# Moving the PSUM evacuation and the squares of y in a two-convolution image kernel, with one more step of lag

## The chip, the cores and the metric

The kernel runs on one core of one Trainium2 chip. The metric is the device time of one execution in microseconds (us); of several executions the median is given, and smaller is better.

## The reference

Eight images of 32 channels and 192 x 192 pixels go through two residual blocks. Each block first normalizes its input over groups of two channels (mean and variance over both planes).

```python
x = x + _L0_conv_ref(_gn(x), w_off, b_off, w_dcn, b_dcn)
x = x + _L1_conv_ref(_gn(x), w1, b1, w2, b2)
# _L0: a 3x3 conv to 2 offsets for each channel, sampling of the plane at the
#      shifted place by bilinear interpolation, then a 3x3 conv over 32 channels
# _L1: pooled = x.mean(axis=(2, 3)); hdn = relu(pooled @ w1 + b1)
#      kernels = (hdn @ w2 + b2).reshape(b, NK, 3, 3); depthwise 3x3 conv with them
```

An offset is below 1 pixel in size, so that the bilinear sample lies between a pixel and one of its direct neighbours in each direction. Which neighbour it is depends on the offset's sign: hence the predicated copies.

## The kernel before

An image is cut into 12 chunks of 16 rows (`CHUNKS = 12`, `TOTAL = 96` chunks in all); 4 rows by 32 channels lie on the 128 partitions, so that a chunk is 4 x 192 elements in each partition. Every engine has its own program, written out as a loop `for i in range(STEPS)`, and semaphores tie them together. Step i of an engine works on several chunks at different distances behind i. A step's number within its image is o = i mod 12, and i = 12 b + o.

TensorE (PE) does in step i: `offsets(i, 0)` and `offsets(i, 1)`, the two halves of the offset convolution into the PSUM tile `z`; `depthwise(i - DW_STEP, 0)`, the second block's convolution into `dw`; `deform(i - 3, 0)`, the first block's second convolution into bank 0 of `dc`; then `depthwise(.., 1)` and `deform(i - 3, 1)` into bank 1. `deform(n, q)` waits on the semaphore `y_done` until bank q has been read out for chunk n - 1. Between these stand a few small matmuls for the statistics of the images: `y_means`, `hidden`, `taps` and `y_bias` (one chain after the last chunk of an image, up to the weights `wy` of the second block), and `x_mean`, `x_var`, `x_biases` for the image to come.

ScalarE (ACT) does in step i: `x_sums` (the sums of one of eight tiles `st` of the next image, loaded by DMA), at times a read of a small result (`read`), then `offset(i, 0)` (tanh of `z` to `du`), `side(i, 0)` (its sign to the mask `mu`), `y_square(i - 4)` (the sum of squares of y over chunk i - 4, which waits for `y_done`), `size(i, 0)`, the same three for the second half (`dv`, `mv`), `finish` for bank 0 of the depthwise result (`ot<-dw`), `sides(i + 1)` (a copy of the neighbours to `nb`), `finish` for bank 1. `depthwise` has one bank `dw` for all but the last image, so each half waits for the `finish` of the half before it.

VectorE (DVE) does in step i `sample(i)` and then `evacuate(i - 3)`. `sample` begins with the large predicated copy (L703, `nb<-mu,xv`, 12 x 190 elements per partition), which needs `mu`; then come two small ones of 768 elements (L710 and L711), which need `mv`, and six tensor_tensor operations up to `sr` (L731). `evacuate(n)` adds `dc`, a bias and the residual into the ring `yr`, for each of two banks, and each time counts `y_done` up by one.

SyncE (SP) issues the DMAs in the order of its own loop: the store of the output, `s_shift`, the loads of x, `st` and the residual, and `y_shift`. GpSimd (POOL) sets borders and does the small arithmetic of the normalizations (`y_norm`, `y_weights`). With `DW_STEP = 19` the second block runs 19 steps behind the first, and `yr` is a ring of `YS = 17` chunks. Steps 0 to 18 have no depthwise work; steps 96 to 114 have no offsets or sampling.

Of the kernel before, what the change touches and what calls it, by code (L numbers as in the profile page):

```python
# [16 lines left out]
B, H, W = 8, 192, 192  # L17
# [10 lines left out]
CNT = HW // G  # L28
STILES = 8
SW = HW // G // STILES  # L30
XS, SS, YS, HS = 3, 3, 17, 4
ABOVE, MID, BELOW = 0, 1, 2
BANK = 512
Q = 2
# [9 lines left out]


DCN_STEP = 3
DW_STEP = 19
STEPS = TOTAL + DW_STEP

TAPS = Q * 2 * 2 * 2  # L50
# [16 lines left out]


def s_dmas(n):
    return 2 + (n % CHUNKS % SS == 0 and n % CHUNKS > 0)  # L70


def r_dmas(n):
# [38 lines left out]
def block_kernel(nc, x, planes, w_off, b_off, w_dcn, b_dcn, w1, b1, w2, b2, consts, xr, out):  # L112
    with ExitStack() as ctx:
# [237 lines left out]
        def _(pe):  # L351
# [112 lines left out]
            def y_means(b):  # L464
                pe.wait_ge(y_tot, b + 1)
                average("ym", b, C_YM, yn[:, 0:2])
# [31 lines left out]
            for i in range(STEPS):  # L498
                b, o = divmod(i, CHUNKS)
                c, d = i - DW_STEP, i - DCN_STEP  # L500
                if i < TOTAL:
                    offsets(i, 0)
                    offsets(i, 1)
                if 0 < b <= B and o == 7:
                    y_bias(b - 1)
                if c >= 0:
                    depthwise(c, 0)
                if 0 <= d < TOTAL:
                    deform(d, 0)
                if 0 < b <= B and o == 5:  # L510
                    taps(b - 1)
                if c >= 0:
                    depthwise(c, 1)
                if 0 <= d < TOTAL:
                    deform(d, 1)
                if 0 < b <= B and o == 3:
                    y_means(b - 1)
                if 0 < b <= B and o == 4:
                    hidden(b - 1)
                if b + 1 < B:  # L520
                    if o == 9:
                        x_mean(b + 1)
                    if o == 10:
                        x_var(b + 1)
                    if o == 11:
                        x_biases(b + 1)

        @block.scalar
        def _(act):
# [122 lines left out]
            for i in range(STEPS):  # L652
                b, o = divmod(i, CHUNKS)
                c, e = i - DW_STEP, i - DCN_STEP - 1
                if b + 1 < B and 0 < o <= STILES:
                    x_sums(b + 1, o - 1)
                    if o == STILES:
                        x_totals(b + 1)
                if 0 < b <= B and o == 4:
                    read("ym", b - 1, mvy[:], sm[:, C_YM:C_YM + 2])  # L660
                if 0 < b <= B and o == 5:
                    hidden_read(b - 1)
                if 0 < b <= B and o == 6:
                    read("tap", b - 1, tapr[:], sm[:, C_TAP:C_TAP + TAPS])
                if b + 1 < B and o == 10:
                    read("xm", b + 1, mx[(b + 1) % 2][:], sm[:, C_XM:C_XM + 1])
                if b + 1 < B and o == 11:
                    read("xv", b + 1, vx[:], sm[:, C_XV:C_XV + 1])
                if 0 < b < B and o == 0:
                    off_bias(b)  # L670
                if i < TOTAL:
                    offset(i, 0)
                    side(i, 0)
                if 0 <= e < TOTAL:
                    y_square(e)
                if 0 < b <= B and o == 3:
                    y_totals(b - 1)
                if i < TOTAL:
                    size(i, 0)
                    offset(i, 1)  # L680
                    side(i, 1)
                    size(i, 1)
                if 0 < b <= B and o == 7:
                    wait(act, o_done, Q * CHUNKS * (b - 1))
                    read("wb", b - 1, wb[:], sm[:, C_WB:C_WB + Q], bias=mvy[:, 0:1])
                    act.wait_ge(small_rd, SMALL["wb", b - 1] + 1)
                if c >= 0:
                    finish(c, 0)
                if i + 1 < TOTAL:
                    sides(i + 1)  # L690
                if c >= 0:
                    finish(c, 1)

        @block.vector
        def _(dve):
            def sample(n):
                b, j = divmod(n, CHUNKS)
                s, v, q, k = n % 2, xv[n % XS], nb[n % 2], s_at(n)
                at = n * LERPS
                dve.wait_ge(sided, n + 1)  # L700
                dve.wait_ge(prepped, 4 * n + 1)
                m3 = mu[s][:].bitcast(U16).unsqueeze(1).to_broadcast([P, 3, NB, W])
                nc.vector.copy_predicated(q[:, :, :, 1:W - 1], m3[:, :, :, 1:W - 1],  # L703
                                          v[:, :, :, 3:W + 1]).then_inc(lerp, 1)
                m1 = mv[s][:].bitcast(U16)
                dve.wait_ge(prepped, 4 * n + 3)
                if j in (0, CHUNKS - 1):
                    dve.wait_ge(mirror, 2 * b + 1 + (j > 0))
                dve.wait_ge(lerp, at + 1)
                nc.vector.copy_predicated(v[:, ABOVE, :, 1:W + 1], m1, v[:, BELOW, :, 1:W + 1]).then_inc(lerp, 1)  # L710
                nc.vector.copy_predicated(q[:, ABOVE], m1, q[:, BELOW]).then_inc(lerp, 1)  # L711


                two, own = q[:, ABOVE:MID + 1], v[:, ABOVE:MID + 1, :, 1:W + 1]
                u2 = du[s][:].unsqueeze(1).to_broadcast([P, 2, NB, W])
                dve.wait_ge(lerp, at + 3)
                nc.vector.tensor_tensor(two, two, own, ALU.subtract).then_inc(lerp, 1)  # L717
                dve.wait_ge(lerp, at + 4)
                dve.wait_ge(prepped, 4 * n + 4)
                nc.vector.tensor_tensor(two, two, u2, ALU.mult).then_inc(lerp, 1)  # L720
                dve.wait_ge(lerp, at + 5)
                nc.vector.tensor_tensor(two, two, own, ALU.add).then_inc(x_free, 1)  # L722
                dve.wait_ge(x_free, n + 1)
                nc.vector.tensor_tensor(q[:, ABOVE], q[:, ABOVE], q[:, MID], ALU.subtract).then_inc(lerp, 1)  # L724
                dve.wait_ge(lerp, at + 6)
                nc.vector.tensor_tensor(q[:, ABOVE], q[:, ABOVE], dv[s][:], ALU.mult).then_inc(lerp, 1)  # L726
                wait(dve, dcn_mm, 2 * (n - 2))
                if n >= SS:
                    dve.wait_ge(s_sh[n % SS], ring(n - SS, SS, s_dmas))
                dve.wait_ge(lerp, at + 7)  # L730
                nc.vector.tensor_tensor(sr[:, k:k + NB, 1:W + 1], q[:, ABOVE], q[:, MID], ALU.add)\  # L731
                    .then_inc(sampled, 1)

            def evacuate(n):
                b, j = divmod(n, CHUNKS)
                k = y_at(n)
                dve.wait_ge(r_in[n % YS], ring(n, YS, r_dmas))
                if j == 0:
                    dve.wait_ge(small_rd, SMALL["ob", b] + 1)
                for q in range(Q):  # L740
                    y = yr[:, k:k + NB, q, 1:PAIRS + 1]
                    dve.wait_ge(dcn_mm, Q * n + q + 1)
                    nc.vector.scalar_tensor_tensor(  # L743
                        out=y, in0=dc[:, q, 0:NB * PAIRS].rearrange("p (k w) -> p k w", w=PAIRS),
                        scalar=db[b % 2][:, q:q + 1], in1=y, op0=ALU.add, op1=ALU.add,
                        accum_out=ys1[b % 2][:, q, j:j + 1]).then_inc(y_done, 1)

            dve.wait_ge(cleared, 4)
            dve.wait_ge(piv, 1)
            for i in range(STILES):  # L750
                dve.wait_ge(first_in[i], 16)
                wait(dve, first_sum, i)
                nc.vector.scalar_tensor_tensor(
                    out=st[0][:], in0=first_tile(yr, i), scalar=npiv[:],
                    in1=zero[:, 0:1].to_broadcast([P, SW]), op0=ALU.add, op1=ALU.add,
                    accum_out=xs1[:, i:i + 1]).then_inc(first_sum, 1)

            for i in range(STEPS):
                if i < TOTAL:
                    sample(i)  # L760
                if 0 <= i - DCN_STEP < TOTAL:
                    evacuate(i - DCN_STEP)

        @block.gpsimd
        def _(pool):
# [161 lines left out]
            for i in range(STEPS):  # L927
# [10 lines left out]
                    set_s_pads(i)  # L938
                if b + 1 < B and o == 0:
                    pivot(b + 1)  # L940
                if 0 < b <= B and o == 4:
                    y_norm(b - 1)
                    set_y_pads(b - 1)
                if b >= 2 and o == 5:
                    set_y_edges(b - 2)
                if 0 < b <= B and o == 6:
                    y_weights(b - 1)
                if b < B and o == 6:
                    edge_weights(b)
# [78 lines left out]
```

## Time and profile before

| | |
|---|---|
| Median of 3 runs | 1628.83 us (1628.58 to 1629.97) |
| Profiled execution, its own time | 1630.0 us |
| Its span on the core | 1628.2 us |
| TensorE matmul busy | 1535.3 us (94%) |
| VectorE busy | 1359.2 us (83%) |
| ScalarE busy | 1053.2 us (65%) |
| GpSimd busy | 326.2 us (20%) |
| Mean busy share of the DMA engines, main queue | 63.0% |

The span runs from the first to the last recorded instruction of the core. A row of the timeline names the start, the length, the engine, the line, the tiles (written before the arrow, read behind it), and in brackets how long the engine had been idle and what released it. Only an idle engine that others wait for costs time, so the shares above don't say by themselves what bounds the kernel: the stages have to be looked at one by one.

### The profile page before, as it was taken

Reading aid. Unit: us, or ns where it says so; the run is one execution under the profiler, and the core shown is the slowest. Engines: PE = TensorE matmul, PEld = TensorE weight load, DVE = VectorE, ACT = ScalarE, POOL = GpSimd, SP = SyncE. Lnnn points to the kernel's source line nnn. Section 1 sums busy time; section 2 is a strip of 40 time slices with the busy share of each in tenths; the row PEclk is TensorE's granted clock in tenths of the full one; section 3 lists DMA queues with packets and bytes.
Section 4 is the critical chain, followed back from the end, with each engine's and each line's share of the span. In section 5 each row is a group of like instructions: output and inputs, shape, how many; then the busy total and the mean of one; then the engine's idle time right before and its main releaser. Section 6 shows DMA issues by size and latency. Waiting matters only on the chain.

```text
span 1628.2 us, 29952 instructions
## 1 busy us (share of the span) xinstructions
PE 1535.3 (94%) x12048; PEld 644.3 (40%) x12048; DVE 1359.2 (83%) x1264; ACT 1053.2 (65%) x1594; POOL 326.2 (20%) x382
## 2 busy tenths in 40 slices
PE   3788888999999999999999999999999999999888
PEld 1333334434444344433444344433444334443343
DVE  3899999988988888899988989898888989889700
ACT  4767567666686667776677666766676665655423
POOL 3000422104030230404121040312304041210010
PEclk9899999999999999999999999999999999999999
DMA  7365455576676658676676766766676765656356
GB/s 243 107 190 176 113 160 176 173 209 178 208 219 201 192 173 237 185 221 191 185 223 199 213 177 209 217 203 192 173 239 187 216 189 158 189 159 199 111 149 218
DMA packets 225274, 307.78 MB, mean 189 GB/s; under 512 B 16656, under 2 KB 167552, under 8 KB 225136
## 3 DMA queue, kind: packets, MB, share of 16 engines
q1 hardware_dynamic: 223632, 304.42, 63.0%
q8 instruction: 95, 1.56, 0.4%
q0 software_dynamic: 1504, 1.45, 0.3%
q14 instruction: 43, 0.35, 0.1%
HBM read 190.18 MB, written 38.14 MB: 140 GB/s over the span
## 4 chain that ended last, share of the span: by engine, by line
PE 65%; DVE 14%; ACT 9%; DMA 4%; issue 4%; SPq 2%; POOL 1%; DVEq 0%; ACTq 0%; POOLq 0%
PE z L357 31%; PE dc L397 16%; PE dw L427 11%; DMA st<-in_planes 3%; DVE nb L722 2%; DVE nb L720 2%; DVE nb L717 2%; ACT dv L536 2%; PE dc L427 2%; ACT mv L543 1%; DVE xv L710 1%; PE dc L401 1%; DVE nb L724 1%; DVE nb L726 1%; DVE nb L711 1%
## 5 line engine op out<-in xcount | busy, mean ns | idle before, releaser
L357 PE MATMUL z<-xv,wos 128*64 128x384 f32 x4608 | 769.2, 490 | 11.1 <-ACT du L536 10.9
L357 PEld LDWEIGHTS z<-xv,wos 128*64 128x64 f32 x4608 | 327.9, 137 | 425.7 <-issue 414.4
L397 PE MATMUL dc<-sr,wds 128*32 128x384 f32 x2304 | 448.2, 520 | 35.8 <-DVE yr L743 35.7
L397 PE MATMUL dc<-sh,wds 128*32 128x384 f32 x2112 | 406.7, 521 | 0.0
L703 DVE COPY_PREDICATED nb<-mu,xv 128x2280 f32<-128x2280 uint16 x96 | 269.6, 2808 | 59.7 <-ACT mu L543 59.1
L427 PE MATMUL dw<-yr,wy 128*64 128x388 f32 x672 | 252.4, 497 | 11.6 <-ACT ot L571 9.2
L427 PE MATMUL dw<-yh,wy 128*64 128x388 f32 x672 | 252.5, 497 | 0.0
L536 ACT ACTIVATE du<-z,ob 128x768 f32<-128x768 f32 x96 | 86.1, 897 | 240.8 <-PE z L357 218.3
L397 PEld LDWEIGHTS dc<-sr,wds 128*32 128x32 f32 x2304 | 122.9, 110 | 298.1 <-issue 297.5
L557 ACT ACTIVATE nb<-xv 128x2292 f32<-128x2292 f32 x96 | 202.6, 2110 | 0.4 <-DVE sr L731 0.3
L710 DVE COPY_PREDICATED xv<-mv,xv 128x768 f32<-128x768 uint16 x96 | 103.1, 1074 | 87.0 <-ACT mv L543 64.5
L722 DVE TENSOR_TENSOR nb<-nb,xv 128x1536 f32<-128x1536 f32 x96 | 169.6, 1766 | 3.3
L720 DVE TENSOR_TENSOR nb<-nb,du 128x1536 f32<-128x1536 f32 x96 | 169.2, 1763 | 3.3
L717 DVE TENSOR_TENSOR nb<-nb,xv 128x1536 f32<-128x1536 f32 x96 | 168.9, 1759 | 3.3
L579 ACT ACTIVATE st<-st,npiv 128x1152 f32<-128x1152 f32 x56 | 70.3, 1256 | 120.8 <-DMA st<-in_planes 98.6
L427 PEld LDWEIGHTS dw<-yr,wy 128*64 128x64 f32 x672 | 83.4, 136 | 151.1 <-issue 93.2
L590 ACT ACTIVATE junk<-yr,nmx 128x768 bf16<-128x768 f32 x96 | 89.4, 931 | 66.3 <-DVE yr L743 66.0
L743 DVE SCALAR_TENSOR_TENSOR yr<-dc,db,yr 128x384 f32<-128x384 f32 x192 | 110.5, 612 | 21.7 <-DMA yr<-in_xr 9.9
L571 ACT ACTIVATE ot<-dw,wb 128x388 f32<-128x388 f32 x168 | 96.6, 575 | 39.8 <-PE dw L427 39.4
L397 PEld LDWEIGHTS dc<-sh,wds 128*32 128x32 f32 x2112 | 113.4, 111 | 3.0 <-issue 3.0
L731 DVE TENSOR_TENSOR sr<-nb 128x768 f32<-128x768 f32 x96 | 93.0, 969 | 12.5
L711 DVE COPY_PREDICATED nb<-mv,nb 128x768 f32<-128x768 uint16 x96 | 100.4, 1046 | 0.0
(118 smaller groups left out, 1586.0 us busy)
## 6 DMA issues: line engine op xcount, KB each, us to landing
xv<-in_x SPq DMA_DIRECT2D x272, 384.0 KB, 4.7
yr<-in_xr SPq DMA_DIRECT2D x96, 392.0 KB, 7.8
out<-ot SPq DMA_DIRECT2D x96, 388.0 KB, 4.3
yh<-yr SPq DMA_DIRECT2D x179, 196.0 KB, 7.2
st<-in_planes SPq DMA_DIRECT2D x56, 576.0 KB, 7.1
sh<-sr SPq DMA_DIRECT2D x160, 194.0 KB, 2.8
sh<-sr SPq DMA_DIRECT2D x32, 145.5 KB, 2.5
yr<-in_planes SPq DMA_DIRECT2D x8, 576.0 KB, 10.3
```

What stands on the lines that cost most here:

```text
L357: last = nc.tensor.matmul(acc[m], weights[:, kx, :], view[:, :, kx:kx + W], start=kx == 0, stop=kx == 2)
L397: last = nc.tensor.matmul(dc[m, q, 0:NB * PAIRS], weights[:, kx, q], view[:, :, cols], start=first, stop=final)
L427: last = nc.tensor.matmul(acc[m], wy[b % 2][:, q, t], view[:, :, t:t + OW], start=t == 0, stop=t == 1)
L536: nc.scalar.activation(d[:].rearrange("p (h k) w -> p h (k w)", h=2), z[:, i, :, 0:HALF * W], ACT.Tanh, bias=ob[b % 2][:, i:i + 1], scale= ...
L557: nc.scalar.activation(nb[s][:, :, :, 1:W], v[:, :, :, 1:W], ACT.Copy)
L703: nc.vector.copy_predicated(q[:, :, :, 1:W - 1], m3[:, :, :, 1:W - 1], v[:, :, :, 3:W + 1]).then_inc(lerp, 1)
L710: nc.vector.copy_predicated(v[:, ABOVE, :, 1:W + 1], m1, v[:, BELOW, :, 1:W + 1]).then_inc(lerp, 1)
L711: nc.vector.copy_predicated(q[:, ABOVE], m1, q[:, BELOW]).then_inc(lerp, 1)
L717: nc.vector.tensor_tensor(two, two, own, ALU.subtract).then_inc(lerp, 1)
L720: nc.vector.tensor_tensor(two, two, u2, ALU.mult).then_inc(lerp, 1)
L722: nc.vector.tensor_tensor(two, two, own, ALU.add).then_inc(x_free, 1)
L743: nc.vector.scalar_tensor_tensor(out=y, in0=dc[:, q, 0:NB * PAIRS].rearrange("p (k w) -> p k w", w=PAIRS), scalar=db[b % 2][:, q:q + 1], i ...
```

## The change

Four things change together. (1) The evacuation that VectorE did at the end of step i - 1 is now done in step i, between the large predicated copy and the two small ones. (2) ScalarE's `y_square`, and `y_totals` with it, go from the middle of the step to its end. (3) Everything in the statistics of the next image's planes (`x_sums`, `x_totals`) and the chain from `y_means` to `y_bias` is one step later. (4) The lag of the second block goes from 19 to 20 steps, and its ring from 17 to 18 chunks. Beside these, the number of DMAs that `s_dmas` gives for the first chunk of an image is 3 in place of 2, which is what `s_shift` issues there.

```diff
-XS, SS, YS, HS = 3, 3, 17, 4
+XS, SS, YS, HS = 3, 3, 18, 4
-DW_STEP = 19
+DW_STEP = 20
 def s_dmas(n):
-    return 2 + (n % CHUNKS % SS == 0 and n % CHUNKS > 0)
+    return 2 + (n % CHUNKS % SS == 0)
...
@@ tensor
-                if 0 < b <= B and o == 7:
+                if 0 < b <= B and o == 8:
                     y_bias(b - 1)
                 if c >= 0:
                     depthwise(c, 0)
                 if 0 <= d < TOTAL:
                     deform(d, 0)
-                if 0 < b <= B and o == 5:
+                if 0 < b <= B and o == 4:
+                    y_means(b - 1)
+                if 0 < b <= B and o == 6:
                     taps(b - 1)
...
-                if 0 < b <= B and o == 3:
-                    y_means(b - 1)
-                if 0 < b <= B and o == 4:
+                if 0 < b <= B and o == 5:
                     hidden(b - 1)
...
@@ scalar
-                if b + 1 < B and 0 < o <= STILES:
-                    x_sums(b + 1, o - 1)
-                    if o == STILES:
+                if b + 1 < B and 1 < o <= STILES + 1:
+                    x_sums(b + 1, o - 2)
+                    if o == STILES + 1:
                         x_totals(b + 1)
...
                 if i < TOTAL:
                     offset(i, 0)
                     side(i, 0)
-                if 0 <= e < TOTAL:
-                    y_square(e)
-                if 0 < b <= B and o == 3:
-                    y_totals(b - 1)
...
                 if c >= 0:
                     finish(c, 1)
+                if 0 <= e < TOTAL:
+                    y_square(e)
+                if 0 < b <= B and o == 3:
+                    y_totals(b - 1)
...
@@ vector
                 nc.vector.copy_predicated(q[:, :, :, 1:W - 1], m3[:, :, :, 1:W - 1],
                                           v[:, :, :, 3:W + 1]).then_inc(lerp, 1)
+                if 0 <= n - DCN_STEP - 1:
+                    evacuate(n - DCN_STEP - 1)
                 m1 = mv[s][:].bitcast(U16)
...
                 if i < TOTAL:
                     sample(i)
-                if 0 <= i - DCN_STEP < TOTAL:
-                    evacuate(i - DCN_STEP)
+                if TOTAL <= i <= TOTAL + DCN_STEP:
+                    evacuate(i - DCN_STEP - 1)
...
@@ gpsimd: y_norm, set_y_pads, set_y_edges and y_weights each one step later
```

VectorE's program in the middle of the kernel, at the joint of two steps. Before, the two evacuations (L743) stand behind the last operation of a sample, ahead of the large copy:

```order
L731 TENSOR_TENSOR sr<-nb 128x4x192 [waits lerp,s_sh2,dcn_mm]
L743 SCALAR_TENSOR_TENSOR yr,ys<-dc,db,yr 128x4x96 [waits dcn_mm,r_in16]
L743 SCALAR_TENSOR_TENSOR yr,ys<-dc,db,yr 128x4x96 [waits dcn_mm]
L703 COPY_PREDICATED nb<-mu,xv 128x12x190 [waits prepped,sided]
L710 COPY_PREDICATED xv<-mv,xv 128x4x192 [waits lerp,prepped]
```

With the change the same two (now L745) stand behind the large copy, which waits for `mu` (semaphore `prepped`):

```order
L733 TENSOR_TENSOR sr<-nb 128x4x192 [waits lerp,s_sh2,dcn_mm]
L703 COPY_PREDICATED nb<-mu,xv 128x12x190 [waits prepped,sided]
L745 SCALAR_TENSOR_TENSOR yr,ys<-dc,db,yr 128x4x96 [waits dcn_mm,r_in14]
L745 SCALAR_TENSOR_TENSOR yr,ys<-dc,db,yr 128x4x96 [waits dcn_mm]
L712 COPY_PREDICATED xv<-mv,xv 128x4x192 [waits lerp,prepped]
```

So the evacuation of a chunk moved behind one more large copy, and behind whatever that copy waits for.

ScalarE's program in a step with a tile of sums, before: the sums (L579, L582) open the step, and the square (L590) stands between the mask `mu` and the second half.

```order
L571 ACTIVATE ot<-dw,wb 128x4x97
L579 ACTIVATE st,xs<-st,npiv 128x1152
L582 ACTIVATE st,xs<-st 128x1152
L615 ACTIVATE tapr<-sm 128x16
L536 ACTIVATE du<-z,ob 128x768
L543 ACTIVATE mu<-du 128x768
L590 ACTIVATE junk,ys<-yr,nmx 128x768
L550 ACTIVATE du<-du 128x768
L536 ACTIVATE dv<-z,ob 128x768
```

With the change, at the same kind of place:

```order
L571 ACTIVATE ot<-dw,wb 128x4x97
L590 ACTIVATE junk,ys<-yr,nmx 128x768
L579 ACTIVATE st,xs<-st,npiv 128x1152
L582 ACTIVATE st,xs<-st 128x1152
L615 ACTIVATE tapr<-sm 128x16
L536 ACTIVATE du<-z,ob 128x768
L543 ACTIVATE mu<-du 128x768
L550 ACTIVATE du<-du 128x768
L536 ACTIVATE dv<-z,ob 128x768
```

The square moved ahead of the sums of the following step, and nothing stands any more between the two halves' activations.

TensorE's program in a step with depthwise work reads alike before and with the change, except for the step from which it holds:

```order
L357 MATMUL z<-xv,wos 64x384 [waits z_read]
L357 MATMUL z<-xv,wos 64x384 x11
L427 MATMUL dw<-yr,wy 64x388 [waits o_done,y_sh2]
L427 MATMUL dw<-yh,wy 64x388
L427 MATMUL dw<-yr,wy 64x388
L427 MATMUL dw<-yh,wy 64x388
L397 MATMUL dc<-sr,wds 32x384 [waits y_done,s_sh2,s_sh1]
```

What moved here is in no row: the `y_done` for which the last of them waits is now given one large copy later.

## Rows read from the trace of the kernel before

**Rows 1.** The page: the span, and each engine's busy time (share) and instructions.
```profile
span 1628.2 us, 29952 instructions
PE 1535.3 (94%) x12048; PEld 644.3 (40%) x12048; DVE 1359.2 (83%) x1264; ACT 1053.2 (65%) x1594; POOL 326.2 (20%) x382
```

**Rows 2.** Busy time in steps 0 to 20, 21 to 95, and the rest.
```profile
core 0: us, PE busy (x) PEld busy (x) DVE busy (x) ACT busy (x) POOL busy (x), PEclk, DMA share, GB/s
29.55:348.39 318.84, 273.00 (x2074) 117.51 (x2067) 285.11 (x253) 214.00 (x306) 49.74 (x53) 0.95 0.52 158
348.39:1533.70 1185.31, 1182.04 (x9378) 490.67 (x9376) 1052.62 (x976) 798.74 (x1205) 253.46 (x271) 1.00 0.67 195
1533.70:1628.20 94.50, 77.01 (x534) 32.96 (x534) 10.10 (x21) 27.70 (x59) 10.47 (x24) 0.95 0.57 173
```

**Rows 3.** The same columns for steps 50, 54, 55 and 59.
```profile
806.38:824.54 18.16, 18.16 (x165) 9.39 (x161) 17.00 (x16) 14.28 (x20) 0.70 (x1) 1.00 0.81 242
872.55:887.62 15.07, 15.07 (x114) 5.76 (x112) 12.11 (x13) 11.43 (x18) 3.66 (x6) 1.00 0.73 212
887.62:903.20 15.58, 15.58 (x133) 6.34 (x129) 14.39 (x15) 10.84 (x16) 0.00 (x0) 1.00 0.74 220
949.08:965.67 16.59, 16.47 (x186) 7.07 (x185) 14.92 (x15) 9.71 (x14) 8.18 (x9) 1.00 0.69 200
```

**Rows 4.** Timeline of step 54, VectorE (start, length, operation).
```profile
875.72 0.61 DVE L743 SCALAR_TENSOR_TENSOR yr<-dc,db,yr 128x384 f32<-128x384 f32 x1
...
878.56 2.80 DVE L703 COPY_PREDICATED nb<-mu,xv 128x2280 f32<-128x2280 uint16 x1 [1.68 <-ACT mu L543]
882.36 1.08 DVE L710 COPY_PREDICATED xv<-mv,xv 128x768 f32<-128x768 uint16 x1 [1.00 <-ACT mv L543]
```

**Rows 5.** Timeline of step 54, ScalarE.
```profile
876.68 0.90 ACT L536 ACTIVATE du<-z,ob 128x768 f32<-128x768 f32 x1 [3.10 <-PE z L357]
877.62 0.84 ACT L543 ACTIVATE mu<-du 128x768 bf16<-128x768 f32 x1
```

**Rows 6.** Timeline of step 54, TensorE: first matmuls of the first deform.
```profile
881.74 0.53 PE L397 MATMUL dc<-sr,wds 128*32 128x384 f32 x2
```

**Rows 7.** Timeline of steps 5 and 6, TensorE and VectorE.
```profile
110.01 2.89 DVE L703 COPY_PREDICATED nb<-mu,xv 128x2280 f32<-128x2280 uint16 x1
113.59 1.05 DVE L710 COPY_PREDICATED xv<-mv,xv 128x768 f32<-128x768 uint16 x1 [0.69 <-ACT mv L543]
...
123.95 0.61 DVE L743 SCALAR_TENSOR_TENSOR yr<-dc,db,yr 128x384 f32<-128x384 f32 x1
...
125.03 2.89 DVE L703 COPY_PREDICATED nb<-mu,xv 128x2280 f32<-128x2280 uint16 x1
```

**Rows 8.** Timeline of TensorE, first deforms of steps 6 and 7.
```profile
124.72 0.55 PE L397 MATMUL dc<-sr,wds 128*32 128x384 f32 x2 [2.75 <-DVE yr L743]
...
129.03 1.19 PE L357 MATMUL z<-xv,wos 128*64 128x384 f32 x6
```

**Rows 9.** Busy time in the first deform of step 7 (columns of rows 2).
```profile
139.70:143.40 3.70, 3.67 (x28) 1.54 (x32) 3.13 (x3) 3.21 (x5) 0.00 (x0) 0.58 0.69 161
```

**Rows 10.** Timeline of ScalarE, waits in steps 2, 6 and 19.
```profile
63.00 1.25 ACT L579 ACTIVATE st<-st,npiv 128x1152 f32<-128x1152 f32 x1 [7.97 <-DMA st<-in_planes]
...
125.14 0.94 ACT L590 ACTIVATE junk<-yr,nmx 128x768 bf16<-128x768 f32 x1 [1.69 <-DVE yr L743]
...
318.13 1.26 ACT L579 ACTIVATE st<-st,npiv 128x1152 f32<-128x1152 f32 x1 [3.69 <-DMA st<-in_planes]
```

**Rows 11.** Timeline of TensorE, the depthwise of step 19 that waits, and the taps of step 53.
```profile
328.13 0.91 PE L427 MATMUL dw<-yr,wy 128*64 128x388 f32 x1 [3.12 <-ACT ot L571]
...
866.96 1.95 PE L479 MATMUL sm<-hid,w2r 128*128 128x2 f32 x16
```

**Rows 12.** Who waited for a tile of the planes, all steps.
```profile
  DMA st<-in_planes: 98.6, 38
```

**Rows 13.** Timeline of ScalarE, one finish in the tail.
```profile
1574.35 0.59 ACT L571 ACTIVATE ot<-dw,wb 128x388 f32<-128x388 f32 x1 [1.63 <-PE dw L427]
```

More of the change, by code:

```diff
@@ L654, in _ @@
                 c, e = i - DW_STEP, i - DCN_STEP - 1
-                if b + 1 < B and 0 < o <= STILES:
-                    x_sums(b + 1, o - 1)
-                    if o == STILES:
+                if b + 1 < B and 1 < o <= STILES + 1:
+                    x_sums(b + 1, o - 2)
+                    if o == STILES + 1:
                         x_totals(b + 1)
-                if 0 < b <= B and o == 4:
+                if 0 < b <= B and o == 5:
                     read("ym", b - 1, mvy[:], sm[:, C_YM:C_YM + 2])
-                if 0 < b <= B and o == 5:
+                if 0 < b <= B and o == 6:
                     hidden_read(b - 1)
-                if 0 < b <= B and o == 6:
+                if 0 < b <= B and o == 7:
                     read("tap", b - 1, tapr[:], sm[:, C_TAP:C_TAP + TAPS])
@@ L682, in _ @@
                     size(i, 1)
-                if 0 < b <= B and o == 7:
+                if 0 < b <= B and o == 8:
                     wait(act, o_done, Q * CHUNKS * (b - 1))
@@ L940, in _ @@
                     pivot(b + 1)
-                if 0 < b <= B and o == 4:
+                if 0 < b <= B and o == 5:
                     y_norm(b - 1)
                     set_y_pads(b - 1)
-                if b >= 2 and o == 5:
+                if b >= 2 and o == 6:
                     set_y_edges(b - 2)
-                if 0 < b <= B and o == 6:
+                if 0 < b <= B and o == 7:
                     y_weights(b - 1)
```

## The prediction

> **What bounds the kernel now.** I read the page first: TensorE is busy for 1535 of 1628 us, VectorE for 83% of it [rows 1]. Then the busy time by stretch, since the work is not the same all through [rows 2]. From step 21 to step 95 TensorE is busy for 1182.0 of 1185.3 us at a granted clock of 1.00: there it alone is the bound, and at most 3.3 us of idle time can be won. In the fill (steps 0 to 20, without depthwise work up to step 18) TensorE has 46 us of idle time in 319, and 17 in the tail. Third, single steps of the long stretch [rows 3]: a plain step is 15.07 us, all of it TensorE's. The step that holds the last chunk of an image in its deform has 18.16, the one with `x_biases` 16.59, the one with `y_bias` 15.58.
>
> Last, where TensorE could come to wait inside such a step. Step 54 begins at 872.55. `du` starts at 876.68, when the first half of `z` is done, `mu` at 877.62 [rows 5], and the large copy at 878.56, after 1.68 us of idle time, so VectorE waits for the mask there and not the other way round [rows 4]. TensorE, never idle, comes to the first deform at 881.74 [rows 6]. The evacuation that this deform needs began at 875.72 [rows 4]: it is some 5 us early, so its place costs nothing before.
>
> In the fill it is VectorE's cycle that counts. Large copies follow each other at 15.02 us (110.01, 125.03), with 0.69 us of idle time ahead of the small copy [rows 7]. That idle time is ScalarE's: `y_square` waits 1.69 us for the evacuation, and the second half's mask stands behind it [rows 10].
>
> **The long stretch: a new wait on TensorE.** Now the evacuation comes after the large copy. In step 54: the copy starts at 878.56 and runs 2.80, to 881.36. An operation without a wait of its own starts a little before the recorded end of the one ahead (two evacuations of 0.61 fill only the 1.08 us from 123.95 to 125.03 [rows 7], 0.07 less each); I take 0.1, so the first evacuation starts at 881.26. From its start to the deform it releases it is 0.77 us: 123.95 to 124.72 [rows 7, 8]. So the deform starts at 882.03 in place of 881.74: 0.29 us of wait. For single steps the copy is 0.02 shorter, and I take 0.27. The copy can't start earlier, whatever VectorE does before it: it starts 0.10 us after the end of `mu` (877.62 + 0.84), and `du`, `mu` follow the first half of `z` without a gap [rows 5]. The second bank has 3 us to spare. Nothing later in the step makes the 0.27 up, since TensorE has no other idle time, so the step is 15.34.
>
> It holds for the 75 steps from 21 to 95, less the six with `y_bias`, which is issued between `z` and the depthwise and delays TensorE's own arrival by 0.5 us, more than the wait: 69 x 0.27 = +18.6 us. Bounds: 0 if the handshake is hidden after all, 0.45 if semaphore and weight load take 0.2 longer behind a short wait.
>
> Against it stands what ScalarE lateness cost: of 98.6 us of waits for the tiles of the planes [rows 12], only part of the 3.3 us of TensorE's idle time is theirs. One step later a tile has been there for a whole step. I take -2.5 (0 to -3.3). `y_square` (0.94 [rows 10], with the read of its accumulator some 1.1) now lies with the sums ahead of `du`; there ScalarE idled 3.10 us [rows 5], so 2.0 us of room are left and `du` stays on time. The ring of 18 for a lag of 20 leaves the residual's load its old distance, so SyncE's queue keeps its order; its tile load for step o waits for sums that are one step later, but these are at the step's head and the load is issued in its middle: nothing. GpSimd has 80% idle time, and its chain shifts as a whole: nothing. The third DMA counted in `s_dmas` was issued before as well and lands two steps ahead of its use: nothing.
>
> **The fill.** VectorE's cycle without the idle time: large copy up to the evacuation 2.76, evacuations 1.08 (123.95 to 125.03), small copy to the end of the sample 10.36 (113.59 to 123.95) [rows 7], 14.20 in all. But now it is chained to TensorE: copy 2.76, handshake 0.77, both deforms 4.31 (124.72 to 129.03 [rows 8]), then `z` up to the next copy 6.01 (872.55 to 878.56 [rows 4]) gives 13.85. So VectorE leads by only 0.35 us, and what TensorE has besides now lengthens the step: the image's last chunk 18.16 - 15.07 - 0.35 = 2.7, `x_biases` 1.52 - 0.35 = 1.2 [rows 3], `taps` 1.95 - 0.35 = 1.6 [rows 11], the small ones 0.5; 6.0 together. Step 20 has the first depthwise: it took long in step 19 before, where `du` was late by the 3.69 us that a tile's DMA took [rows 10] and TensorE then waited 3.12 us for a `finish` [rows 11]; without that it is 15.58 + 0.27, say 15.8 [rows 3].
>
> The large copy of step 5, at 110.01 before, I put at 109.0: the wait of 7.97 us in step 2 [rows 10] goes, which is worth 1.7, and one evacuation less stands ahead; but TensorE then waits long for the first evacuation and comes back at the low clock. Then 14 x 14.20 = 198.8 to the copy of step 19, 6.0 of extra work, 7.8 to the next `z`, 15.8: step 21 begins at 337.4 in place of 348.4, **-11.0 us**. Bounds: -4 (more steps at the low clock) and -16 (none, and a quick start).
>
> The clock is the fill's unknown. In step 7 TensorE idled 2.7 us and then ran its deform at a granted clock of 0.58, partly at 1.2 in place of 2.4 GHz [rows 9]; in step 6, after 2.75 us, it did not [rows 8]. The idle piece is now 1.9 us.
>
> **The tail.** One more chunk of depthwise work is left after step 95. There the halves alternate with ScalarE on one bank at 1.63 + 0.59 = 2.2 us each [rows 13]: +4.4. (If it hid behind something, +2.6, its matmuls alone.)
>
> **Sum.** -11.0 + 18.6 - 2.5 + 4.4 = +9.5 us. The profiled execution had 1630.0 us (span 1628.2 and 1.8 around it), the median of the runs is 1628.83, 1.2 less: forecast 1638.3, about 1638. A measurement of this kernel tells a change of 0.2%, 3.3 us, from none.
>
> **The rivals.** *The evacuation is hidden (faster).* The deform's wait overlaps with the pipeline of the depthwise ahead of it, so that nothing is lost. For it: TensorE's weight loads run ahead, and 0.27 us is less than one matmul (0.53 [rows 6]). Against: the 0.77 us is measured at the matmul itself. Then -11.0 - 2.5 + 4.4 = -9.1: 1620. It decides below (11.0 + 2.5 - 4.4) / 69 = 0.13 us of wait per step. Chance 0.15.
>
> *Little of each (no change):* a wait of 0.08 to 0.18 us per step, or a fill that gains 5 us more. Chance 0.07.
>
> *ScalarE late (much slower).* Before, a late `du` was covered by the evacuation's 5 us; now every late us of `mu` is one of TensorE's. If the tile loads still come late, or `y_square` waits, at 0.3 us a step on average, 75 x 0.3 = +22 more: 1660. Against it: the 2.0 us of room above. Chance 0.08.
>
> *The clock falls in the long stretch.* The granted clock is 1.00 where TensorE is never idle [rows 2], and fell in step 7 behind an idle piece [rows 9]. If the new short waits made it fall once a step as there (3.70 us at 0.58, so 1.55 us lost), it would be 75 x 1.55 = +116: about 1755. The Trainium skill (TensorE: Matmul & The Clock Gate, section "A second HAM failure mode: psum-queue depth-cycling") tells of a kernel whose short idle pieces between groups of matmuls made the clock go to and fro, which speaks for this rival; no row here has such short idle pieces in every step, so the trace can't confirm it. Chance 0.02.
>
> **Numbers.** The forecast has 0.68. Its own bounds, 0.15 to 0.40 us of wait and -14 to -6 in the fill, give 1627 to 1652; the range 1627 to 1650 leaves out the hidden case and the two dear ones and holds about 0.8. Faster by over 0.2% 0.15, within it 0.07, slower 0.78.
>
> **What would show it.** Right: in steps 21 to 95 TensorE waits for `yr` in nearly every step for 0.2 to 0.35 us, a plain step is 15.3 to 15.4 us, that stretch is 1200 us or more, the large copy starts 6.0 us after `z`, VectorE's idle time ahead of the small copy is gone; the fill ends near 337; the wait for planes' tiles is nearly zero. Wrong: plain steps still of 15.07 us, or waits for `yr` of over 0.5 us; a fill that ends after 344 or before 332; low clock in the long stretch.

## The result: slower by 0.5%, 1636.25 us

The changed kernel's median is 1636.25 us (5 runs, 1633.49 to 1640.56) against 1628.83 us (5 runs, 1627.22 to 1629.97). The ratio is 1.005, with a 95% interval of 1.0027 to 1.0072: it is slower. Its profiled execution had 1633.49 us, the fastest of the five.

The page of the changed kernel, and its busy time in the same three stretches as [rows 2] (steps 0 to 20, 21 to 95, the rest):

```profile
span 1631.7 us, 29947 instructions
PE 1528.6 (94%) x12048; PEld 649.2 (40%) x12048; DVE 1356.5 (83%) x1264; ACT 1056.3 (65%) x1594; POOL 314.7 (19%) x380
```

```profile
core 0: us, PE busy (x) PEld busy (x) DVE busy (x) ACT busy (x) POOL busy (x), PEclk, DMA share, GB/s
29.55:334.16 304.61, 260.62 (x2095) 113.57 (x2087) 283.19 (x253) 211.01 (x297) 55.64 (x52) 0.97 0.53 161
334.16:1533.16 1199.00, 1185.06 (x9378) 499.21 (x9376) 1051.88 (x976) 803.76 (x1213) 236.65 (x272) 1.00 0.66 193
1533.16:1631.70 98.54, 80.14 (x551) 33.80 (x550) 10.03 (x21) 28.75 (x61) 10.34 (x24) 0.94 0.57 174
```

The fill ends 14.2 us earlier (334.16 for 348.39), the long stretch is 13.7 us longer, the tail 4.0 us longer: +3.5 us of span. The shares of busy time on the page hardly moved; only the split into stretches shows that two large effects of opposite sign nearly cancel.

TensorE had 3.3 us of idle time in the long stretch before; now it is 13.9. What ended it, from the list of waits of that stretch, for TensorE alone (total us, times, longest):

```profile
PE dc L397 <- DVE yr L745: 13.6, 69, 0.4
PE sm L460 <- issue: 0.2, 1, 0.2
```

That is 69 waits for an evacuation, 0.2 us each: one in each of the 75 steps but the six with `y_bias`. In step 54, beginning at 862.37, the rows that answer to [rows 4 to 6] are these, of VectorE, ScalarE and TensorE in turn:

```profile
868.39 2.83 DVE L703 COPY_PREDICATED nb<-mu,xv 128x2280 f32<-128x2280 uint16 x1 [1.61 <-ACT mu L543]
871.11 0.60 DVE L745 SCALAR_TENSOR_TENSOR yr<-dc,db,yr 128x384 f32<-128x384 f32 x1
...
872.19 1.08 DVE L712 COPY_PREDICATED xv<-mv,xv 128x768 f32<-128x768 uint16 x1
```

```profile
866.51 0.90 ACT L536 ACTIVATE du<-z,ob 128x768 f32<-128x768 f32 x1 [2.32 <-PE z L357]
867.44 0.84 ACT L543 ACTIVATE mu<-du 128x768 bf16<-128x768 f32 x1
```

```profile
871.87 0.53 PE L397 MATMUL dc<-sr,wds 128*32 128x384 f32 x2 [0.23 <-DVE yr L745]
```

The large copy starts 6.02 us into the step, where it did before (6.01), the evacuation at 8.74, and the deform 0.76 us after it, at 9.50 in place of 9.19. ScalarE has 2.32 us to spare ahead of `du`, so it isn't late.

The deform comes 0.31 us later, yet only 0.23 us of idle time is recorded ahead of it. Before, it started while the last matmul ahead of it was still recorded as running (881.32 to 881.81, the deform at 881.74). That overlap is lost behind a wait, and it shows as busy time: 1185.06 us in the long stretch, where e1 below, without these waits, has 1180.80. So the cost of the waits is read from the length of the stretch, not from the idle time alone.

Single steps, to be read against [rows 3]: steps 50, 55, 56 and 59 (55 is a plain one now, and 56 has `y_bias`).

```profile
797.14:815.55 18.41, 18.22 (x165) 9.40 (x161) 16.99 (x17) 13.08 (x19) 1.94 (x1) 1.00 0.81 240
...
879.59:894.87 15.28, 15.11 (x117) 5.92 (x113) 12.10 (x13) 11.63 (x18) 2.18 (x4) 1.00 0.74 211
894.87:910.40 15.53, 15.53 (x133) 6.27 (x129) 14.19 (x15) 11.84 (x18) 0.00 (x0) 1.00 0.75 215
941.87:958.61 16.74, 16.50 (x186) 7.23 (x185) 14.77 (x14) 9.61 (x15) 7.78 (x10) 1.00 0.60 178
```

A plain step is 15.28 for 15.07 us, the one with the last chunk 18.41 for 18.16, the one with `x_biases` 16.74 for 16.59, and the one with `y_bias` 15.53 for 15.58: of these it alone didn't get longer, since TensorE comes later to its deform by itself.

In the fill, VectorE (compare [rows 7]):

```profile
106.43 2.75 DVE L703 COPY_PREDICATED nb<-mu,xv 128x2280 f32<-128x2280 uint16 x1 [0.80 <-ACT mu L543]
109.08 0.60 DVE L745 SCALAR_TENSOR_TENSOR yr<-dc,db,yr 128x384 f32<-128x384 f32 x1
...
110.23 1.08 DVE L712 COPY_PREDICATED xv<-mv,xv 128x768 f32<-128x768 uint16 x1
...
120.64 2.75 DVE L703 COPY_PREDICATED nb<-mu,xv 128x2280 f32<-128x2280 uint16 x1
```

Copy follows copy at 14.21 us for 15.02; the idle time ahead of the small copy is gone.

### The profile page after: what moved, and what is told of

The parts are those of the page before. It is cut to its first block, busy times and chain, and to the rows that moved or that the text cites. A ratio compares the mean times of both kernels' runs of the same rounds, so it can differ in the third digit from the quotient of the medians.

```text
span 1631.7 us, 29947 instructions
## 1 busy us (share of the span) xinstructions
PE 1528.6 (94%) x12048; PEld 649.2 (40%) x12048; DVE 1356.5 (83%) x1264; ACT 1056.3 (65%) x1594; POOL 314.7 (19%) x380
## 4 chain that ended last, share of the span: by engine, by line
PE 63%; issue 14%; DVE 13%; ACT 8%; DMA 1%; POOL 0%; SPq 0%; DVEq 0%; ACTq 0%; POOLq 0%
PE z L357 25%; PE dc L397 22%; PE dw L427 9%; ACT du L536 3%; ACT mu L543 3%; DVE nb L703 2%; PE dc L427 2%; DVE nb L724 2%; DVE nb L722 2%; DVE nb L719 2%; DVE yr L745 2%; PE dc L401 2%; PE dc L406 1%; DVE nb L726 1%; DVE xv L712 1%
## 5 line engine op out<-in xcount | busy, mean ns | idle before, releaser
L397 PE MATMUL dc<-sr,wds 128*32 128x384 f32 x2304 | 441.3, 512 | 55.7 <-DVE yr L745 55.7
L397 PE MATMUL dc<-sh,wds 128*32 128x384 f32 x2112 | 399.4, 514 | 0.0
L397 PEld LDWEIGHTS dc<-sr,wds 128*32 128x32 f32 x2304 | 131.8, 109 | 309.4 <-issue 308.2
L536 ACT ACTIVATE dv<-z,ob 128x768 f32<-128x768 f32 x96 | 86.5, 901 | 125.0 <-PE z L357 125.0
L745 DVE SCALAR_TENSOR_TENSOR yr<-dc,db,yr 128x384 f32<-128x384 f32 x192 | 110.1, 611 | 22.9 <-DMA yr<-in_xr 10.3
L733 DVE TENSOR_TENSOR sr<-nb 128x768 f32<-128x768 f32 x96 | 93.2, 971 | 12.5
L726 DVE TENSOR_TENSOR nb<-nb 128x768 f32<-128x768 f32 x96 | 92.8, 966 | 3.3
```

Of the source, the lines that this page charges most:

```text
L397: last = nc.tensor.matmul(dc[m, q, 0:NB * PAIRS], weights[:, kx, q], view[:, :, cols], start=first, stop=final)
L536: nc.scalar.activation(d[:].rearrange("p (h k) w -> p h (k w)", h=2), z[:, i, :, 0:HALF * W], ACT.Tanh, bias=ob[b % 2][:, i:i + 1], scale= ...
L745: nc.vector.scalar_tensor_tensor(out=y, in0=dc[:, q, 0:NB * PAIRS].rearrange("p (k w) -> p k w", w=PAIRS), scalar=db[b % 2][:, q:q + 1], i ...
```

## The experiments

The theory: TensorE's first deform now hangs on ScalarE's mask, the large copy and an evacuation, with nothing in between, and this wait is the whole loss of the long stretch; the fill gains from the square's place and the later sums. The main rival: the loss comes from ScalarE's new order, the chain's new places or the lag, or from any operation put between the copies. Ratios are to runs of the kernel before on the same chip, with their 95% intervals.

### e1_evac_home: the evacuation back at the end of the step

```diff
@@ vector, against the changed kernel
-                if 0 <= n - DCN_STEP - 1:
-                    evacuate(n - DCN_STEP - 1)
...
-                if TOTAL <= i <= TOTAL + DCN_STEP:
-                    evacuate(i - DCN_STEP - 1)
+                if 0 <= i - DCN_STEP < TOTAL:
+                    evacuate(i - DCN_STEP)
```

> The changed kernel with the evacuation put back to the end of the step; ScalarE's squares at the end, the later sums and chain and the lag of 20 stay. If the wait behind the large copy is the cause of the loss: plain steps of the long stretch go from 15.30 back to 15.07 us, steps 21 to 95 take 1183 to 1186 us, and the fill gets shorter too, since VectorE's cycle of 14.2 us is no longer chained to TensorE's (step 21 begins near 329 in place of 334); with a tail of 98.5 that is a span of about 1611 and a time of 1612 to 1615, below both kernels. If instead the late square, the chain's new places or the lag cost TensorE its time in the long stretch: it stays near 1199 us and the time above 1628.

1615.53 us, ratio 0.9904 (0.9884 to 0.9924). Its stretches:

```profile
29.50:333.23 303.73, 263.95 (x2055) 113.98 (x2050) 285.02 (x253) 210.76 (x297) 52.46 (x50) 0.96 0.53 161
333.23:1514.85 1181.62, 1180.80 (x9378) 490.55 (x9376) 1052.62 (x976) 799.52 (x1213) 242.42 (x272) 1.00 0.67 196
1514.85:1613.50 98.65, 80.11 (x551) 33.68 (x550) 10.09 (x21) 28.76 (x61) 10.39 (x24) 0.94 0.56 174
```

The long stretch loses 17.4 us (1199.00 to 1181.62), 0.25 for each of the 69 waits, and TensorE's idle time there is 0.8 us. This part of the rival is out: square, sums, chain and lag cost TensorE nothing in it. The tail is that of the changed kernel within 0.1 us. Where the expectation missed is the fill: it ends at 333.2, not 329, and the time is 0.5 us above the expected range. VectorE's cycle is longer than 14.2 us with the evacuation at the end:

```profile
107.82 2.90 DVE L703 COPY_PREDICATED nb<-mu,xv 128x2280 f32<-128x2280 uint16 x1
110.83 1.07 DVE L710 COPY_PREDICATED xv<-mv,xv 128x768 f32<-128x768 uint16 x1
...
122.27 2.93 DVE L703 COPY_PREDICATED nb<-mu,xv 128x2280 f32<-128x2280 uint16 x1
```

That is 14.45: the large copy takes 2.90 here (2.75 in the fill of the changed kernel), and the small copy starts 0.1 us behind the end of the large one, for whose signal it waits, where the evacuation covered this. So VectorE's edit does save some 0.24 us per step where VectorE is the bound; over 14 steps that is 3.4 of the 4 us missed, and the copy of step 5 starts 1.4 us later than in the changed kernel (107.82 for 106.43).

### e2_bank0_first: bank 0 at the end, bank 1 between the copies

```diff
@@ vector, against the changed kernel (evacuate takes a bank, and waits for the residual with bank 0)
                if 0 <= n - DCN_STEP - 1:
-                    evacuate(n - DCN_STEP - 1)
+                    evacuate(n - DCN_STEP - 1, 1)
...
                 if TOTAL <= i <= TOTAL + DCN_STEP:
-                    evacuate(i - DCN_STEP - 1)
+                    evacuate(i - DCN_STEP - 1, 1)
+                if 0 <= i - DCN_STEP < TOTAL:
+                    evacuate(i - DCN_STEP, 0)
```

> The changed kernel with the evacuation cut in two: bank 0 at the end of the step, bank 1 between the large and the small copies. If only bank 0's signal is late (TensorE asks for bank 1 some 3 us after it is given): the wait in the long stretch goes as with both at the end, plain steps of 15.07 us, 1612 to 1618 us in all. If any evacuation between the copies costs (the port, a longer copy, a late small copy): plain steps of 15.2 us or more and over 1625 us.

1612.48 us, ratio 0.9886 (0.9868 to 0.9904). Its fill and long stretch, and VectorE at the joint of steps 51 and 52:

```profile
29.80:330.61 300.81, 264.21 (x2059) 109.41 (x2053) 283.33 (x253) 210.91 (x297) 58.88 (x50) 0.97 0.54 163
330.61:1512.51 1181.90, 1180.80 (x9378) 490.69 (x9376) 1052.20 (x976) 799.50 (x1213) 255.85 (x272) 1.00 0.67 196
```

```profile
825.28 0.61 DVE L746 SCALAR_TENSOR_TENSOR yr<-dc,db,yr 128x384 f32<-128x384 f32 x1
...
826.13 2.78 DVE L703 COPY_PREDICATED nb<-mu,xv 128x2280 f32<-128x2280 uint16 x1 [0.23 <-ACT mu L543]
828.80 0.61 DVE L746 SCALAR_TENSOR_TENSOR yr<-dc,db,yr 128x384 f32<-128x384 f32 x1
...
829.93 1.07 DVE L712 COPY_PREDICATED xv<-mv,xv 128x768 f32<-128x768 uint16 x1 [0.52 <-ACT mv L543]
```

An evacuation still stands between the copies, and TensorE loses nothing (1181.90 us in the long stretch): it is bank 0's signal alone that was late, not the place as such. (e12_bank0_again below is the same kernel on another chip.)

### e3_evac_after_small: the suspected wait made longer

```diff
@@ vector, against the changed kernel
-                if 0 <= n - DCN_STEP - 1:
-                    evacuate(n - DCN_STEP - 1)
...
                 nc.vector.copy_predicated(q[:, ABOVE], m1, q[:, BELOW]).then_inc(lerp, 1)
+                if 0 <= n - DCN_STEP - 1:
+                    evacuate(n - DCN_STEP - 1)
```

> The changed kernel with the evacuation behind the two small copies, so 3.0 us later in the step (small copies from 9.82 to 11.8 us after the first z). If TensorE's first deform hangs on it with nothing in between, it starts at 12.5 us in place of 9.45: plain steps of 18.3 us, the long stretch 1199 + 75 x 3.0 = 1425 us, the fill 45 us longer, about 1900 us in all. If part of the latency is hidden or a deform has other slack: clearly less than 3.0 us per step, under 1850.

2029.43 us (one run). Its long stretch, then steps 45 and 46 (beginning at 904.38 and 924.61), and TensorE's deform in step 45:

```profile
416.95:1932.24 1515.29, 1276.49 (x9378) 527.38 (x9376) 1037.81 (x976) 804.60 (x1213) 147.46 (x272) 0.93 0.52 153
904.38:924.61 20.23, 17.11 (x119) 6.63 (x115) 14.12 (x15) 11.47 (x20) 0.52 (x3) 0.92 0.49 144
924.61:943.22 18.61, 15.48 (x116) 6.21 (x115) 12.36 (x12) 9.23 (x13) 3.34 (x8) 1.00 0.54 150
```

```profile
916.77 0.55 PE L397 MATMUL dc<-sr,wds 128*32 128x384 f32 x2 [3.12 <-DVE yr L745]
```

The deform starts at 12.39 us into the step, 12.5 expected, and step 46, whose granted clock is 1.00, takes 18.61 (it holds `x_var`, 0.3 us): the delay of 2.9 us reaches the step's length in full. In the long stretch TensorE waits 75 times for `yr`, 238.6 us together. The time is above the 1900 us expected; what the expectation left out is TensorE's clock: most other steps take near 20 us at a granted clock of 0.92. The long stretch grew by 316 us, of which 75 x 2.9 = 218 is the wait; the granted clock of 0.93 in 1515 us means 212 us at 1.2 in place of 2.4 GHz, so 106 us lost (an estimate). These two make 324. The fill grew by 83 us (its end 416.95 for 334.16) where 45 were expected.

### e4_vector_alone: VectorE's edit without ScalarE's

The edit is VectorE's part of the change, on the kernel before.

> The kernel before with VectorE's edit alone. ScalarE's square stays in the middle and now waits for an evacuation that stands behind the large copy of the same step; the mask mv stands behind the square. VectorE's cycle would be 2.8 copy + 1.1 evacuations + 0.1 + 1.1 square + 0.75 + 0.9 + 0.85 + 0.1 + 10.4 = 18.0 us in all of the steps 4 to 95: 95 + 92 x 18.0 + 90, about 1840 us. If the square's place did not matter it would be as the changed kernel, 1630 to 1640.

1988.15 us (one run). Two rows of its list of waits, and its steps 45 and 46:

```profile
ACT junk L590 <- DVE yr L745: 410.2, 96, 7.9
...
PEld dw L427 <- ACT ot L571: 263.4, 80, 4.5
```

```profile
876.33:894.90 18.57, 15.55 (x118) 6.25 (x115) 12.79 (x13) 8.94 (x12) 0.00 (x0) 1.00 0.50 140
894.90:915.01 20.11, 17.18 (x115) 6.49 (x115) 15.44 (x15) 9.23 (x13) 8.91 (x8) 0.92 0.52 146
```

The square waits for the evacuation as expected. The expectation of 1840 counted VectorE's cycle alone; in fact TensorE is stopped as well, since `finish` stands behind the late square on ScalarE and the second half of the depthwise waits for it (203.7 us over steps 21 to 95, once in each), and its clock falls in most steps. So the two edits depend on each other: the evacuation could only go between the copies because the square left the middle.

### e5_lag19_home and e6_lag19_bank0: the lag of 19 with a packed chain

Both are the kernel before with the squares at the end of the step and the later sums (and the count in `s_dmas`); e6 has the banks split as e2 has.

```diff
@@ tensor, against the kernel before (y_means and hidden no longer end steps 3 and 4)
+                if 0 < b <= B and o == 4:
+                    y_means(b - 1)
+                if 0 < b <= B and o == 5:
+                    hidden(b - 1)
                 if 0 < b <= B and o == 7:
                     y_bias(b - 1)
@@ scalar: the reads "ym" and "hid" of steps 4 and 5 stand ahead of the read "wb", not at the head
```

> The kernel before (lag 19, ring 17, evacuation at the end of the step) with the squares at the end, the sums one step later, and the chain packed so that it ends in its old steps: y_means and hidden stand right behind the offsets of steps 4 and 5, their reads in the middle of ScalarE's step. If the lag costs one chunk of depthwise in the tail, as forecast (4.4 us): the tail is 94.5 in place of 98.5 us and the time some 4 us below the run with the lag of 20, 1610 to 1613. If the packed chain makes TensorE wait (y_means for the totals, hidden for y_norm): up to 2 us per image more in the long stretch and 1615 to 1630.

> The same as e5_lag19_home with bank 0 evacuated at the end of the step and bank 1 between the copies. If bank 1 between the copies only helps VectorE's cycle in the fill (14.2 in place of 14.4 us per step): some 3 us less than e5_lag19_home, 1606 to 1611. If that difference was the clock's chance: the same as e5_lag19_home within 1 us.

e5: 1618.51 us, 0.9932 (0.9914 to 0.9950). e6: 1615.24 us, 0.9909 (0.9878 to 0.9939). The saving of a chunk in the tail did not come: e5 is not below e1, whose interval (on another chip) overlaps its own. e6 is above the 1606 to 1611 us expected. The long stretch and tail of e5:

```profile
333.31:1517.10 1183.79, 1182.65 (x9378) 489.38 (x9376) 1053.80 (x977) 800.64 (x1213) 250.10 (x274) 1.00 0.67 196
1517.10:1616.70 99.60, 79.44 (x534) 33.44 (x534) 10.13 (x21) 27.83 (x59) 10.44 (x24) 0.91 0.53 164
```

The long stretch is 2.2 us longer than e1's. The packed chain is seen in it: step 5 of an image, which now holds both `hidden` and `taps`, takes 17.6 us in the mean, where it took 17.0 in the kernel before. What the lag has to do with the 2.2 us isn't separated. In the tail TensorE has 20.2 us of idle time (18.5 in e1, with one chunk more) and a clock of 0.91. e6 is 3 us under e5, as the split banks promised, but the two intervals overlap, so this isn't shown.

### e11_lag19_tail and e12_bank0_again

e11 is e6 with the chain and squares of the last image back in the places of the kernel before; e12 is e2's kernel on the same chip.

```diff
@@ tensor, against e6
-                if 0 < b <= B and o == 4:
+                if 0 < b < B and o == 4:
                     y_means(b - 1)
...
                     deform(d, 1)
+                if b == B and o == 3:
+                    y_means(b - 1)
+                if b == B and o == 4:
+                    hidden(b - 1)
@@ scalar: y_square, y_totals and the reads in the same manner
```

> e6_lag19_bank0 with the chain and the squares of the last image (steps 96 and up) in the places of the kernel before, since without offsets nothing hides the packed chain there. If the packed chain is what kept the lag of 19 from saving its chunk in the tail: the depthwise of the last image begins some 67 us after the first z of step 95 in place of 69 to 72, the tail is 93 to 96 us, and the time is 2 to 4 us below e12_bank0_again on the same chip. If the tail is only the clock's chance: no difference beyond 1.5 us.

> The kernel of e2_bank0_first once more, beside e11_lag19_tail on one chip: 1611 to 1616 us, ratio to the kernel before 0.988 to 0.991, plain steps of 15.07 us again.

e11: 1610.82 us, 0.9874 (0.9859 to 0.9889). e12: 1612.34 us, 0.9877 (0.9858 to 0.9895). Tail of e11, and of e12:

```profile
1513.81:1609.20 95.39, 75.88 (x534) 32.96 (x534) 10.11 (x21) 27.70 (x59) 10.45 (x24) 0.96 0.56 171
```

```profile
1514.63:1617.90 103.27, 82.04 (x551) 35.23 (x550) 10.09 (x21) 28.75 (x61) 10.40 (x24) 0.92 0.54 166
```

In e11 the last image's depthwise begins 67.9 us after the first `z` of step 95, in e12 after 72.7 (kernel before 67.0, changed kernel 71.6): the lag is worth its chunk there. But the timed difference is 1.5 us, below the 2 to 4 expected and with intervals that overlap, since e11 pays 2.2 us in the long stretch (1184.03 for 1181.82), and since the tail of one kernel differs by 3.5 us between two runs on two chips (99.8 in e2 at a granted clock of 0.93, 103.3 in e12 at 0.92). Both beat the kernel before by 1.2%; which is better is not settled.

### e7_square_alone and e8_sums_alone: the two sources of the gain

e7 is e5 with the sums in their old steps; e8 is the kernel before with this alone:

```diff
@@ scalar, against the kernel before
-                if b + 1 < B and 0 < o <= STILES:
-                    x_sums(b + 1, o - 1)
-                    if o == STILES:
+                if b + 1 < B and 1 < o <= STILES + 1:
+                    x_sums(b + 1, o - 2)
+                    if o == STILES + 1:
                         x_totals(b + 1)
```

> e5_lag19_home with the sums in their old steps: of the changes to the kernel before only the squares' place (and the packed chain that it needs) is left. If the idle time ahead of the small copy was the square's wait: the fill's cycle goes from 15.03 to 14.4 us, step 21 begins near 340 in place of 348, the long stretch stays at 1185, and the time is 1618 to 1622. If the fill's gain was from the later sums instead: 1626 to 1630 here.

> The kernel before with the sums of the next image's planes one step later, and nothing else. If they only took away waits for a tile's DMA: 1.7 us in step 2, some 3 in step 19, 1 to 2.5 in the long stretch, so 1622 to 1626. If those waits lay beside other work: 1627 to 1630, as before.

e7: 1621.85 us, 0.9943 (0.9926 to 0.9961); its fill ends at 339.26, as expected. e8: 1626.18 us, 0.9977 (0.9965 to 0.9989), fill and long stretch each 2 to 3 us shorter than before:

```profile
346.25:1528.66 1182.41, 1181.45 (x9378) 490.23 (x9376) 1052.54 (x976) 800.51 (x1211) 256.74 (x274) 1.00 0.67 196
```

Both gain, the square 9 us (with the packed chain and the count that come with it in e7) and the sums 4.

### e9_lag_alone and e10_count_alone

e9 is the changed kernel with VectorE's edit, the square's place and the later sums undone, e10 the kernel before with the count in `s_dmas` alone.

> The changed kernel with VectorE's edit, the square's place and the later sums undone: against the kernel before, the lag of 20, the ring of 18 and the chain a step later are left (and the count in s_dmas). If the lag costs a chunk of depthwise in the tail: 98.5 in place of 94.5 us there; in the fill the first depthwise comes one step later, worth 0 to 4 us; the long stretch 1185: 1629 to 1633 in all. If the lag also pays in the fill for what it costs: 1626 to 1629.

> The kernel before with the corrected count of DMAs in s_dmas alone. The copies it counts land two steps ahead of their use, so no difference is expected: within 2 us of the kernel before. If TensorE or VectorE had relied on the loose wait: a wait on sh of 1 us or more in each image, over 1636.

e9: 1633.60 us, 1.0008 (0.9998 to 1.0019). e10: 1630.33 us, 0.9989 (0.9977 to 1.0000). No cost of the count shows; its interval just reaches 1. The tails of e9 and of e10:

```profile
1531.19:1631.60 100.41, 79.59 (x550) 34.32 (x550) 10.07 (x21) 28.88 (x61) 10.42 (x24) 0.94 0.55 170
```

```profile
1532.98:1632.10 99.12, 78.38 (x534) 33.90 (x534) 10.11 (x21) 27.72 (x59) 10.48 (x24) 0.93 0.54 165
```

e10 does the same work in the tail as the kernel before, and takes 99.12 us for 94.50 [rows 2]. So the tail of the kernel before was a short one, and a difference of 4 us between two single tails can be chance. The lag costs between nothing and 3 us in all: its tail is long, but the long stretch of e9 came out at 1183.15 us, 2 us below before (and 1 below e10, 1184.31). What made it shorter I have not separated.

## Why the prediction was right

Each step of the sum against what was measured:

- **The wait in the long stretch, +18.6 (69 x 0.27).** Shown: 69 waits, and 17.4 us by putting the evacuation back, 0.25 each. Two of the signs named were missed by a hair: the recorded waits are 0.197 us in the mean (0.2 to 0.35 named) and the stretch 1199.0 us (1200 or more). The parts fit as well: copy at 6.02, evacuation to deform 0.76 (0.77 forecast), no wait in the steps with `y_bias`. e2 shows that it is bank 0's signal, and e3 that 2.9 us more of delay are 2.9 us more of step.
- **ScalarE no longer late, -2.5.** It measured -3.7 (1185.31 to 1181.62 in e1), slightly more than the 3.3 us of idle time that I took as its bound, and TensorE's busy time fell as well (1182.04 to 1180.80); e8 alone gives -2.9. No tile of the planes is waited for any more, where it was 98.6 us before [rows 12]: the group of their sums reads

```profile
L579 ACT ACTIVATE st<-st,npiv 128x1152 f32<-128x1152 f32 x56 | 69.7, 1245 | 0.0
```

- **The fill, -11.0.** It measured -14.2. VectorE's cycle was forecast at 14.20 and is 14.21; from the copy of step 5 to that of step 19 it was to be 204.8 us, and is 204.2 (106.43 to 310.65, from the trace); step 20 takes 15.85 for 15.8. The term off is the start: the copy of step 5 is at 106.4, not 109.0. The later sums alone bring it to 107.7 (e8), 2.3 us where I counted 1.7, and the evacuation that no longer stands ahead of it is 1.1. That makes 3.4 of the 3.6 us (110.01 to 106.43), so that the low clock, which I had set against them, cost nothing that shows here. The fill's unknown went well, too: from that copy to step 21 the granted clock is 1.00 (0.96 before), with waits of TensorE of 2.4 us at most (3.4 before). That what TensorE has besides now lengthens steps of the fill is seen too: the step with the last chunk takes 16.90 us there, in place of the common 14.1. But the forecast's implied alternative, that the fill would gain more without the chaining, fell with e1: it ends at 333.2, where VectorE's own cycle is longer by as much.
- **The tail, +4.4.** It measured +4.0, and the last image's depthwise starts 4.6 us later after step 95. The agreement is in part luck: e10, with the same tail as the kernel before, has 99.1 us there and a depthwise 1.8 us later, so that a single pair of tails doesn't settle 4 us. As a timed whole the lag is worth less: 1.3 us, interval -0.3 to +3.1 (e9).
- **The sum, +9.5.** By spans it is +3.5; by medians +7.4. Stage by stage the forecast was 3.2 us too high in the fill, 2.4 in the long stretch (+16.1 for +13.7) and 0.4 in the tail. That the median lies only 2.1 us from the forecast is therefore in part luck. The profiled execution was the fastest of five: 1633.49 us at a mean granted clock of 0.991, against 1640.56 at 0.988. A mean lower by 0.003 over 1635 us is 10 us at half speed, so some 5 us lost (an estimate), most of that difference. The Trainium skill (TensorE: Matmul & The Clock Gate, section "What's actually happening") says that the number of slow matmuls at one kernel's start varies from run to run; the five mean clocks differ in this way too (0.988 to 0.991). In the one run that has a trace the low pieces lie in the fill before the copy of step 5 (0.89 from 29.55 to 106.43) and in the tail (0.94); where the others have theirs, no trace shows.

Of the rivals, the hidden evacuation is out (69 waits), and the late ScalarE too (2.32 us to spare in step 54). The falling clock didn't come in the changed kernel: 1.00 over the long stretch in spite of the 69 short waits. It came in e3 and e4, where TensorE stands still for some 3 us in every step (0.93 in e3). The Trainium skill (TensorE: Matmul & The Clock Gate, section "A second HAM failure mode: psum-queue depth-cycling") tells of a kernel whose clock went to and fro with frequent short idle pieces. This case shows both sides: with one piece of 0.2 us in nearly every step the granted clock stayed at 1.00, with one of some 3 us it fell.

So the change is two gains, a small cost and one large loss. Against the kernel before: the square's place (e7) -9 us, the later sums (e8) -4, the lag about +1, and on top of them VectorE's edit, +18 us by spans (1631.7 against 1613.5) and +21 by medians (1636.25 against 1615.53, on two chips; +24 by the ratios to the kernel before on each chip, 1.005 and 0.9904). The first three add up to -12, and without VectorE's edit the same kernel measured 1% (16 us) less than before; where the other 4 us are from I have not separated.

## What to carry to other kernels

An operation of an engine that isn't the bound may still carry the signal that the bound engine waits for. Before moving it, count the chain from the bound engine's own output through all that now stands ahead of it and back, and compare with the moment at which the bound engine asks: here (step 54) 9.50 us into the step against 9.19, and 0.25 us in 69 steps outweighed both gains. Splitting the operation, so that the part with the early signal stays early and the rest fills the gap, kept the gains and not the loss. And an idle gap on an engine may be caused by an operation on another (here the square on ScalarE): take away the cause before filling the gap.

## What was unexpected of the hardware

In the fill (steps 5 to 19) the large predicated copy takes 2.89 us in the mean in e1, where an evacuation stands ahead of it, and 2.75 in the changed kernel, where a tensor_tensor does; its inputs are the same. The operation ahead doesn't explain it by itself: in the long stretch the same two orders take 2.79 both. What runs beside the copy differs as well (TensorE is busy for 2.90 of the 2.90 us of the copy at 107.82 in e1, and for 1.94 of the 2.75 us of that at 106.43 in the changed kernel), and I have not tested which of these it is. And TensorE's clock is a cost on its own once a wait per step is long: in e3 a third of the growth of the long stretch, 106 of 316 us by the estimate above, is time lost at the lower level.
